# A graph-attention and similarity kernel on one core: output product in three one-pass products, normalisations moved to GpSimd, a residual added by an accumulating load

## What is computed

```python
# first layer
h = x @ W_fc.T;  f1 = h @ a1;  f2 = h @ a2
attn = softmax(where(adj == 0, -1e9, leaky_relu(f1[:, None] + f2[None, :], 0.2)), axis=-1)
y = x + elu(attn @ x)
xl = (y - mean(y)) / sqrt(var(y) + 1e-5)
# second layer
xn = xl / sqrt(max(sum(xl * xl), 1e-12))
y2 = xl + (xn @ xn.T @ adj) @ xl
out = (y2 - mean(y2)) / sqrt(var(y2) + 1e-5)
```

## Time and profile before

| | |
|---|---|
| time, median of 3 runs | 348.49 us (347.63 to 349.29) |
| time of the profiled execution | 350.04 us |
| its span in the trace | 348.2 us |
| busy: PE, PEld | 311.9 us (90%), 297.4 us (85%) |
| busy: DVE, ACT, POOL | 281.1 us (81%), 295.4 us (85%), 212.2 us (61%) |
| DMA | 42.43 MB, 122 GB/s over the span |

### The profile page before, as it was taken

One profiled execution on the slowest core, in us unless ns is written; L12 is line 12 of the kernel. 1 busy time (PEld: TensorE's weight loads), 2 busy tenths in 40 slices (PEclk: granted clock), 3 DMA queues, 4 the chain that ended last, 5 costly groups with the idle time before them and its releaser, 6 DMA issues.

```text
span 348.2 us, 7246 instructions
## 1 busy us (share of the span) xinstructions
PE 311.9 (90%) x2372; PEld 297.4 (85%) x2372; DVE 281.1 (81%) x996; ACT 295.4 (85%) x609; POOL 212.2 (61%) x231
## 2 busy tenths in 40 slices
PE   3076699999999999999999999999999999997880
PEld 1065699999999999999999999999999999996860
DVE  3278988989898989899898989898989988766231
ACT  1399797999999999999999999999999999945242
POOL 3212757685967676666668596767666677655301
PEclk9999999999999999999999999999999999999697
DMA  6961044255464464553634545446355252101011
GB/s 199 287 182 36 27 123 121 60 161 144 122 180 124 128 175 125 142 161 72 188 107 162 142 122 174 128 126 180 121 132 172 73 171 62 56 7 60 2 60 60
DMA packets 33972, 42.43 MB, mean 122 GB/s; under 512 B 1136, under 2 KB 25744, under 8 KB 33936
## 3 DMA queue, kind: packets, MB, share of 16 engines
q0 software_dynamic: 16896, 25.17, 26.5%
q1 hardware_dynamic: 17040, 16.81, 15.5%
HBM read 33.59 MB, written 8.39 MB: 121 GB/s over the span
## 4 chain that ended last, share of the span: by engine, by line
PE 80%; POOL 6%; issue 5%; DMA 4%; DVE 2%; ACT 1%; SPq 0%; ACTq 0%; POOLq 0%; DVEq 0%
PE ps_l L711 15%; PE ps_l L673 9%; PE ps_l L674 9%; PE ps_h L643 8%; PE ps_h L644 8%; PE ps_h L645 8%; PE ps_probT L627 7%; PE ps_l L697 4%; PE ps_l L699 4%; PE ps_l L698 4%; PE ps_l L683 4%; DMA x_hi<-x 3%; PE ps_f L616 2%; POOL y L228 1%; POOL x_lo L221 1%
## 5 line engine op out<-in xcount | busy, mean ns | idle before, releaser
L643 PE MATMUL ps_h<-x_hi,probT_hi 128*128 128x256 f32 x256 | 78.4, 306 | 3.1 <-ACT y L517 2.1
L644 PE MATMUL ps_h<-x_lo,probT_hi 128*128 128x256 f32 x256 | 71.5, 279 | 0.0
L645 PE MATMUL ps_h<-x_hi,probT_lo 128*128 128x256 f32 x256 | 71.4, 279 | 0.0
L673 PE MATMUL ps_l<-xn_hi,adj_sb 128*128 128x256 f32 x256 | 66.3, 295 | 3.1 <-POOL xn_lo L261 3.1
L674 PE MATMUL ps_l<-xn_lo,adj_sb 128*128 128x256 f32 x256 | 64.8, 289 | 0.0
L711 PE MATMUL ps_l<-w_sb,xnT 128*128 128x256 f32 x256 | 62.9, 380 | 0.3
L261 POOL TENSOR_TENSOR xn_lo<-xn,xn_hi 128x1024 fp32r<-128x1024 f32 x16 | 38.5, 2404 | 37.1 <-ACT xn_hi L525 37.1
L643 PEld LDWEIGHTS ps_h<-x_hi,probT_hi 128*128 128x128 f32 x256 | 48.2, 188 | 7.1 <-DVE probT_lo L363 3.3
L673 PEld LDWEIGHTS ps_l<-xn_hi,adj_sb 128*128 128x128 f32 x256 | 50.8, 198 | 3.9 <-issue 3.5
L627 PE MATMUL ps_probT<-ident,prob 128*128 128x128 f32 x256 | 39.4, 278 | 13.6 <-ACT prob L491 12.9
L674 PEld LDWEIGHTS ps_l<-xn_lo,adj_sb 128*128 128x128 f32 x256 | 50.8, 198 | 0.0
(11 more groups left out here) (57 smaller groups left out, 775.0 us busy)
## 6 DMA issues: line engine op xcount, KB each, us to landing
adj_sb<-adj POOLq DMA_DIRECT2D x16, 1024.0 KB, 6.0
x_sb<-x SPq DMA_DIRECT2D x16, 512.0 KB, 4.6
x_hi<-x POOLq DMA_DIRECT2D x16, 512.0 KB, 4.0
out<-o_sb SPq DMA_DIRECT2D x16, 512.0 KB, 3.1
attn_cols<-w_attn SPq DMA_DIRECT2D x2, 0.1 KB, 1.6
wfc<-w_fc SPq DMA_DIRECT2D x1, 32.0 KB, 1.7
```

Source lines behind the costliest of these rows:

```text
L643: nc.tensor.matmul(ps, probT_hi[:, c, blk], x_hi[n][:, k, :], start=(k == 0), stop=False)
L644: nc.tensor.matmul(ps, probT_hi[:, c, blk], x_lo[n][:, k, :], start=False, stop=False)
L645: last = nc.tensor.matmul(ps, probT_lo[:, c, blk], x_hi[n][:, k, :], start=False, stop=(k == NC - 1))
L673: nc.tensor.matmul(ps, a, xn_hi[n][:, k, :], start=(k == 0), stop=False)
```

## The change

Six things change together.

1. **Output product.** ACT writes the transposed tile and w as `xnT_hi` and `w_hi` in the one-pass type, DVE adds two functions `xnT_lo_part` and `w_lo_part` that write the low parts, and `make_out` does three one-pass products for each d in place of one fp32 product.
2. **First normalisation** goes from DVE to POOL (`normalise`, four instructions of 128x256).
3. **Second normalisation** goes from ACT to POOL (`normalise2`, four instructions of 128x256, in the form subtract mean, multiply by scale, so that the small instructions for the negated mean and the bias go).
4. **Residual x.** POOL issues a DMA that adds x from HBM onto `y`, which holds the relu part (`add_x`); DVE's `residual` goes.
5. **ELU rest.** ACT computes relu(1 - exp) in one instruction of 128x1024 (`elu_rest`), and POOL subtracts it from y (`residual`).
6. **Order.** All five loops are written in a new order, and SP's reload of x_sb waits for the last readers that are left (`node_scores` and `split_x`).

The core of the diff:

```diff
+            def add_x(g):
+                ...
+                pool.wait_ge(elu_ok, NC * (g + 1))
+                pool.dma_start(y[n][:], x_rows[g], accum_op=ALU.add).then_inc(yx_in[n], 16)
+
+            def residual(g):
+                ...
+                pool.wait_ge(yx_in[n], 16 * (r + 1))
                 pool.wait_ge(q_ok, g + 1)
-                pool.tensor_tensor(y[n][:], y[n][:], exp_h[:], ALU.add).then_inc(y_ok, 1)
+                pool.tensor_tensor(y[n][:], y[n][:], exp_h[:], ALU.subtract).then_inc(y_ok, 1)
...
+            def normalise(g):
+                ...
+                pool.wait_ge(powers_ok, g + 1)
+                if graph(g - NBUF):
+                    pool.wait_ge(y2_ok, NC * (g - NBUF + 1))
+                for c in range(NC):
+                    last = pool.tensor_scalar(xn[n][:, c, :], y[n][:, c, :], mv[n][:, c, 0:1], powers[n][:, 1, c:c + 1],
+                                              ALU.subtract, ALU.mult)
+                last.then_inc(xn_ok, 1)
...
+            def normalise2(g):
+                ...
+                for c in range(NC):
+                    last = pool.tensor_scalar(o_sb[:, c, :], y2[n][:, c, :], mv2[n][:, c, 0:1], scale2[n][:, c:c + 1],
+                                              ALU.subtract, ALU.mult)
+                last.then_inc(o_ok, 1)
...
-            def residual(g):
-                ...
-                dve.wait_ge(elu_ok, NC * (g + 1))
-                nc.vector.scalar_tensor_tensor(out=exp_h[:], in0=exp_h[:], scalar=1.0, in1=x_sb[n][:],
-                                               op0=ALU.min, op1=ALU.add).then_inc(q_ok, 1)
...
+            def xnT_lo_part(g, d):
+                ...
+                nc.vector.tensor_tensor(xnT_lo[:, d, :], ps_l1[(XT0 + d) % 3][:], xnT_hi[:, d, :].bitcast(F32),
+                                        ALU.subtract).then_inc(xnT_ok, 1)
+
+            def w_lo_part(g, d):
+                ...
+                nc.vector.tensor_tensor(w_lo[:, d, :], ps_l1[(W0 + d) % 3][:, 0:D], w_hi[:, d, :].bitcast(F32),
+                                        ALU.subtract).then_inc(w_ok, 1)
...
+            def elu_rest(g):
+                ...
+                nc.scalar.activation(exp_h[:], exp_h[:], ACT.Relu, bias=1.0, scale=-1.0).then_inc(q_ok, 1)
...
-                    last = nc.tensor.matmul(ps, xnT[:, d, c * P:(c + 1) * P], w_sb[:, d, :], start=(d == 0),
-                                            stop=(d == DC - 1))
+                    blk = slice(c * P, (c + 1) * P)
+                    nc.tensor.matmul(ps, xnT_hi[:, d, blk], w_hi[:, d, :], start=(d == 0), stop=False)
+                    nc.tensor.matmul(ps, xnT_hi[:, d, blk], w_lo[:, d, :], start=False, stop=False)
+                    last = nc.tensor.matmul(ps, xnT_lo[:, d, blk], w_hi[:, d, :], start=False, stop=(d == DC - 1))
```

More of the change, by code:

```diff
@@ L110, in program @@
         adj_in = [sem(f"adj_in{n}") for n in range(NBUF)]
+        yx_in = [sem(f"yx_in{n}") for n in range(NBUF)]
         out_stored = sem("out_stored")
@@ L282, in shift2 @@
                 pool.wait_ge(scale2_ok, g + 1)
-                pool.tensor_tensor(bias2[n][:], scale2[n][:], neg_mean2[n][:], ALU.mult).then_inc(norm2_ok, 1)
-            for i in STEPS:
-                norm(i)
-                split_xn(i)
-                load_x_hi(i + 2)
-                shifted_moments2(i - 1)
-                power2(i - 1)
-                load_adj(i + 3)
-                residual_sum(i + 1)
-                shift2(i - 1)
-                split_x(i + 2)
-                shifted_moments(i + 1)
-                power(i + 1)
+                if graph(g - 1):
+                    pool.wait_ge(out_stored, 16 * g)
+                for c in range(NC):
+                    last = pool.tensor_scalar(o_sb[:, c, :], y2[n][:, c, :], mv2[n][:, c, 0:1], scale2[n][:, c:c + 1],
+                                              ALU.subtract, ALU.mult)
+                last.then_inc(o_ok, 1)
+            for i in STEPS:
+                shifted_moments(i - 2)
+                power(i - 2)
+                normalise(i - 2)
+                split_xn(i - 2)
+                add_x(i - 1)
+                norm(i - 2)
+                split_x(i)
+                shifted_moments2(i - 3)
+                power2(i - 3)
+                load_adj(i + 1)
+                residual(i - 1)
+                normalise2(i - 3)
+                load_x_hi(i + 2)
         @block.vector
@@ L380, in row_moments @@
                     dve.wait_ge(mv_ok, g)
+                if graph(g - NBUF):
+                    dve.wait_ge(xn_ok, g - NBUF + 1)
                 for c in range(NC):
@@ L387, in row_moments @@
                 last.then_inc(mv_ok, 1)
-            def normalise(g):
-                if not graph(g):
-                    return
-                n = g % NBUF
-                dve.wait_ge(powers_ok, g + 1)
-                for c in range(NC):
-                    last = nc.vector.tensor_scalar(xn[n][:, c, :], y[n][:, c, :], mv[n][:, c, 0:1],
-                                                   powers[n][:, 1, c:c + 1], ALU.subtract, ALU.mult)
-                last.then_inc(xn_ok, 1)
             def z_lo_part(g, c):
@@ L518, in elu_relu @@
                                      scale=rden[n][:, c:c + 1]).then_inc(elu_ok, 1)
+            def elu_rest(g):
+                if not graph(g):
+                    return
+                act.wait_ge(elu_ok, NC * (g + 1))
+                nc.scalar.activation(exp_h[:], exp_h[:], ACT.Relu, bias=1.0, scale=-1.0).then_inc(q_ok, 1)
             def xn_hi_part(g):
@@ L544, in copy_xnT @@
                     act.wait_ge(o_ps, NC * g)
-                nc.scalar.activation(xnT[:, d, :], ps_l1[(XT0 + d) % 3][:], ACT.Copy).then_inc(xnT_ok, 1)
+                nc.scalar.activation(xnT_hi[:, d, :], ps_l1[(XT0 + d) % 3][:], ACT.Copy).then_inc(xnT_hi_ok, 1)
             def copy_w(g, d):
@@ L550, in copy_w @@
                 act.wait_ge(w_ps, DC * g + d + 1)
-                nc.scalar.activation(w_sb[:, d, :], ps_l1[(W0 + d) % 3][:, 0:D], ACT.Copy).then_inc(w_ok, 1)
-            def normalise2(g):
-                if not graph(g):
-                    return
-                n = g % NBUF
-                act.wait_ge(norm2_ok, g + 1)
-                if graph(g - 1):
-                    act.wait_ge(out_stored, 16 * g)
-                for c in range(NC):
-                    last = nc.scalar.activation(o_sb[:, c, :], y2[n][:, c, :], ACT.Identity,
-                                                bias=bias2[n][:, c:c + 1], scale=scale2[n][:, c:c + 1])
-                last.then_inc(o_ok, 1)
@@ L565, in _ @@
[L565 to L596 removed]
+                nc.scalar.activation(w_hi[:, d, :], ps_l1[(W0 + d) % 3][:, 0:D], ACT.Copy).then_inc(w_hi_ok, 1)
@@ new lines, in _ @@
+            for i in STEPS:
+                scale_z(i - 3, 1)
+                softmax_exp(i - 1, 1)
+                scale_z(i - 3, 2)
+                probT_hi_part(i - 1, 0)
+                lrelu(i - 1, 2)
+                scale_z(i - 3, 3)
+                probT_hi_part(i - 1, 1)
+                copy_xnT(i - 3, 0)
+                softmax_exp(i - 1, 2)
+                lrelu(i - 1, 3)
+                copy_xnT(i - 3, 1)
+                softmax_exp(i - 1, 3)
+                probT_hi_part(i - 1, 2)
+                copy_w(i - 3, 0)
+                elu_exp(i - 1, 0)
+                elu_relu(i - 1, 0)
+                elu_exp(i - 1, 1)
+                probT_hi_part(i - 1, 3)
+                elu_relu(i - 1, 1)
+                copy_w(i - 3, 1)
+                make_mask(i)
+                xn_hi_part(i - 2)
+                elu_exp(i - 1, 2)
+                elu_relu(i - 1, 2)
+                lrelu(i, 0)
+                elu_exp(i - 1, 3)
+                elu_relu(i - 1, 3)
+                elu_rest(i - 1)
+                lrelu(i, 1)
+                scale_z(i - 2, 0)
+                softmax_exp(i, 0)
```

132 lines of the change are left out of this document (58 added, 74 removed).

## The result

The changed kernel takes **482.34 us** (median of 4 runs, 480.49 to 488.09); the kernel before took 348.06 us beside it. The ratio is 1.383, 95% interval 1.377 to 1.390: 38% slower. The run of 488.09 us had a lower granted clock (0.72 against 0.87) and is left out of the ratio. I had forecast 366 us in a range of 345 to 392. The direction was right, the size was wrong.

The account below looks back on a forecast made before the run. PE bounded the kernel before; POOL was to bound it after, at 19.6 us per graph against 18.83. Periods +10.8, start +4.3, last interval +2.2, end -0.2 made +17.1 us: 366 us, range 345 to 392.

Parts of the forecast that it names:

- the price p: Time of one 128x256 tensor-scalar on POOL: between 0.53 and 0.87 us, taken as 0.53.
- The sum for the loop: POOL's queue per graph: 15.4 us plus 4.2 for the eight new instructions, 19.6 us, above PE's 18.2.
- POOL's wait for z at the load of adj: POOL's load of adj needs all four z tiles; PE makes them in 3.8 us, so no wait.
- PE's part: Split output product on PE: 24 one-pass products take 2.81 us, saving 0.67 and leaving 18.2 us per graph.
- the load hidden in the loop: Accumulating load lands after 4.0 us under 6.2 us of other POOL work, costing only its 0.85 issue.
- Start and last interval: Outside the steady loop: +4.3 us before the first make_z, +2.2 us in the last interval.
- the middle price of my third rival: Accumulating load slow, at the 6.0 us of adj's load: only the ends move, 370 us; slow case 0.12.
- The one in which PE stays the bound: Tensor-scalars at or below 0.35 us keep POOL's loop within PE's 18.2; 344 to 351 us, chance 0.26.
- The one in which a column costs as two-input work: POOL's tensor-scalar at 0.87 us, period 22.4, about 406 us; chance 0.08.
- The slow load: Accumulating load at 8.0 us, twice x_hi's: every period 1.8 longer, each end 4.0, 399 us; chance 0.12.
- DVE late at y: Late y holds up DVE's row moments and then PE, which becomes the bound: 380 us; chance 0.04.
- the signs that I had named: Profile: POOL instructions 0.53 apart, period 19.6, PE waiting over 1 us, ACT and DVE under 90%, make_z near 49.

Follow-up runs that it names:

- experiment 1: Small bench kernel without the model: POOL runs blocks of single instruction forms alone, then beside DVE; 244.11 us in all.
- experiment 7: Changed kernel with each group of four POOL tensor-scalars replaced by two 128x1024 tensor-tensors with a broadcast second operand; 431.52 us, ratio 1.238.
- experiment 9: Changed kernel with 64 extra transposes of the identity on PE ahead of each graph's make_z; 469.28 us, ratio 1.344.
- experiment 6: Changed kernel with each of POOL's eight tensor-scalars on 64 of its 256 columns; 393.38 us, ratio 1.129.
- experiment 11: Kernel before with only the residual changed: x by accumulating load, ELU rest on ACT, x_lo ahead of POOL's subtraction; 399.94 us, ratio 1.145.
- experiment 5: Changed kernel with the first normalisation back on DVE, right behind w's low parts, and the second on ACT at its step's end; 378.27 us, ratio 1.083.
- experiment 10: Kernel before with only the output product split into three one-pass products, low parts on DVE; 367.31 us, ratio 1.052.

## Why the prediction was wrong

**The step that failed** is the price p of a tensor-scalar of 128x256: "At most it is that of the two-input instruction". The bound took a column at 2.17 ns at most, and I chose 0.53 us from the memset's slope. Alone on the chip it is 1.21 us (experiment 1), beyond both ends of 0.53 to 0.87, in place 1.21 (xn) and 1.41 (o_sb). The argument for the bound was that only one tensor is read. It doesn't hold: for 1024 columns the tensor-scalar takes 3779 ns and the two-input add 2337 (experiment 1), and two passes of another form are quicker in place (experiment 7). What I lacked was a row: no large tensor-scalar on POOL stood in the trace of before. The small ones of 128x4 could not tell the slope, and the memset and the two-input add were other forms. The honest upper bound was open.

The rule of the Trainium skill that I weighed (GPSIMD Engine Reference, Engine selection), by which one-input work runs roughly at line rate on GpSimd, is not what these runs show: 128x256 takes 1.21 us with two operations and 0.84 with one and a constant, four to six times the 0.21 us that I estimated by that rule.

**The sum for the loop.** The prediction had 15.4 + 4.2 = 19.6. Measured is 27.3:

- the eight, 10.5 in place of 4.2: +6.3, of which 8 x (1.21 - 0.53) = 5.4 is the form alone, by experiment 1, and some 0.8 is o_sb's excess in place;
- POOL's wait for z at the load of adj, put at nothing: +1.2. I took PE's z at full clock (3.8 us), though I had forecast a wait of PE just ahead of it. Experiment 9 shows that the clock is the cause: with PE kept busy all but a fifth of this wait goes, and 13 us with it;
- the rest of the queue, 15.9 in place of 15.4: +0.4, from the accumulating load's issue (215.78 to 216.69, 0.91) and nrm_sq, which takes 0.69 behind it.

These make 27.5. That POOL's in-order sum sets the period was right, and it held for eight short instructions too (experiment 6). PE's part was right, by its timeline in the changed kernel (three of the tiles, of six products each):

```profile
234.04 0.28 PE L740 MATMUL ps_l<-w_hi,xnT_hi 128*128 128x256 f32 x1
...
236.08 0.28 PE L742 MATMUL ps_l<-w_hi,xnT_lo 128*128 128x256 f32 x1
```

The 18 products from the first line to the last start 0.12 us apart, so a tile takes 0.72 us, and 0.70 was forecast. Right were also the wait for xn_hi (1.17 for 1.2), the moments covered by o_sb, and the load hidden in the loop (5.9 us under 6.2 of other work, and more now).

**Start and last interval.** Forecast +4.3 and +2.2, measured +9.9 and +9.0. DVE's residual of the first graph in the kernel before, then POOL's timeline in the changed one, first and last graph:

```profile
31.31 1.23 DVE L371 SCALAR_TENSOR_TENSOR exp_h<-exp_h,x_sb 128x1024 f32<-128x1024 f32 x1 [0.22 <-ACT y L517]
```

```profile
33.00 1.32 POOL L232 DMA_DIRECT2D y<-x  x1 [17.31 <-ACT y L551]
...
38.92 2.37 POOL L240 TENSOR_TENSOR y<-y,exp_h 128x1024 f32<-128x1024 f32 x1 [1.49 <-DMA y<-x]
...
436.00 2.39 POOL L240 TENSOR_TENSOR y<-y,exp_h 128x1024 f32<-128x1024 f32 x1 [2.83 <-DMA y<-x]
438.37 4.86 POOL L309 TENSOR_SCALAR o_sb<-y,mv,scale 128x256 f32<-128x256 f32 x4
...
445.62 4.86 POOL L267 TENSOR_SCALAR xn<-y,mv,powers 128x256 f32<-128x256 f32 x4
```

The first load is issued at 33.00, 1.7 us after the point where DVE's residual began before; that part comes from the first layer in its new order and I had left it out. From the issue to y is 5.9 us, not 0.85 + 4.0: the adding load took as long as adj's with twice the bytes, as the middle price of my third rival had it. The four xn cost 5.5 at the start and 4.86 at the end in place of 2.1. In the last interval o_sb stands on the path between y and POOL's moments, 4.86 us, where DVE's row moments take 1.8; with the 2.1 that I had taken for it, it would have been all but covered.

**The rivals.** The one in which PE stays the bound falls with p. The one in which a column costs as two-input work (406 us, chance 0.08) was the nearest, but still too cheap: by its own law, 15.4 + 8p with p = 1.3 gives 25.8. The slow load happened only in its mild form, at the ends. DVE late at y was not what bound PE, though DVE waits 21.3 us for y in the whole run; in another order, experiment 11, that wait grows to 66.4 us, 4 of a period of 21.8. Of the signs that I had named, PE's wait (over 1 us), ACT and DVE under 90% and the 0.70 of the output product came out; the spacing of 0.53, which I had called decisive, did not, nor what hangs on it (the period, and make_z's first start, 54.9 in place of 49).

**What the rest of the change is worth.** Without the two normalisations on POOL it still costs 29 us (experiment 5). The split product alone costs 19 (experiment 10), where 0.67 us of PE are bought with 2.2 of DVE. What the accumulating load, the ELU rest on ACT and the new order cost each, no run separates. I found no version that beats the kernel before. In those tried DVE (experiment 10) or ACT (experiment 5, busy 187.23 of 200 us) has 19.3 us of work per graph, over the 18.85 of the period before; but the periods are 20.14 and 20.57, and what makes up the 0.8 and 1.3 us between is not shown. In experiment 5 the chain that ended last lies for 42% on POOL and 24% on DVE.

## What to carry to other kernels

Before work is moved to an engine with room, its price there has to come from a row of that very form (operation, shape, kind of operand), or be measured by a kernel of a few lines; a bound from "it reads less" isn't one. When an engine in order becomes the bound, its period is the sum of its queue with the waits in it, and one more item in a queue should be placed where neither its own wait nor what it pushes back closes a circle with the other queues. TensorE, when it has to wait, may come back at half its clock, and then the engine that it waited for waits for it in turn (experiment 9).
